# Two attentions of a four-layer kernel: the dilated shift moved into spare rows of the queries, and weighted sums turned by transpositions

## The chip, the cores and the metric

The kernel runs on one core of one Trainium2 chip. The core has five instruction streams that run side by side: PE (TensorE, which multiplies matrices; its loads of the standing operand are listed as PEld), DVE (VectorE), ACT (ScalarE), POOL (GpSimd) and SP (SyncE, which here only issues transfers). The metric is the device time of one execution in microseconds (us); lower is better.

## The reference, cut to what matters

The input is x with 8 batches of 512 tokens of 128 numbers. Four layers follow, each added to x. The first and the third are attentions with 16 heads of 8 numbers:

```python
# layer 1 (called "w" in the kernel): three attentions over the same q, k, v, averaged
o_loc = attention within windows of 128 tokens
o_dil = attention among the tokens i, i+4, i+8, ... (DIL = 4 phases of 128 tokens)
o_glb = attention over all 512 tokens
o = (o_loc + o_dil + o_glb) / 3 @ w_out
# layer 3 (called "c"): q and k rotated (RoPE), causal attention over 512 tokens
```

Layers 2 and 4 are mixtures of experts; the change doesn't touch them.

## The kernel before, in words

One function, `attention`, builds both attentions (`causal` False for the first, True for the second). A batch is cut into four groups of four heads; one group of one batch is a slot, and there are 32 slots in each attention. The order of the work inside a slot is written out by hand in `slot`, the same list for every engine: unit i (10 units in the first attention, 8 in the second) is one `scores` of that unit, then the products for maxima (`smax`) of a later slot, then whatever `put(i, ...)` places there. Every engine walks the list in order and waits on semaphores, so a late operand stops all that stands behind it on that engine.

**Queries and keys.** To keep precision in bf16, q and k are split into three bf16 parts each. `parts_out` writes the parts of a batch from SBUF to a scratch tensor in DRAM, and `stacks` reads them back so that the tiles QS and KS hold 72 rows (3 x 3 x 8) whose product is q times k. Rows 72 to 95 are zero. Rows 96 to 110 of QS hold the shifts (in three bf16 parts) that are taken off the scores before the exponential: for each window block and, as the fifth, for the dilated attention. KS rows 96 to 127 hold marks that pick the right shift row for a key block. `smax` multiplies rows 0 to 95 alone; DVE then takes the maxima, and `maxima` (DVE, POOL), `rows` (PE transposes them, ACT copies them to the tile MR, SP moves MR to QS rows 96 and on) make the shifts of the next slot. The first `scores` of a slot waits for that transfer (semaphore `s_ml`).

**Scores.** In the first attention units 0 to 7 multiply all 128 rows; units 8 and 9 make the dilated scores of two heads each: for each head one product of `dil_b` (a constant with ones at the fifth shift rows) with all of QS, 128x512, which lays the dilated shift down in PSUM, then four products of rows 0 to 95, 128x128 each, added to it.

**Sums.** `pv` multiplies exponentials by values into one PSUM bank, 32 rows a head: in the first attention the rows 10k to 10k+8 of a head are the eight sums and the denominator of kind k (local, dilated, global parts), in the second rows 0 to 8. `evac` (ACT) copies the bank to the tile OS. `sel` then turns it to tokens: PE multiplies OS by a constant `pick` (four float32 products of 108 columns in the first attention, 36 in the second), and DVE divides by the denominators and writes PR (POOL adds the three kinds) or ON.

**SP's order around the change.** In a slot with g = 1 of the first attention SP issues, one behind the other, `rows`, then `parts_out(b+1, 1)` (three transfers), and then, at the start of the slot with g = 2, `stacks(b+1, 0)` and `stacks(b+1, 1)` (six transfers each). PE needs the first of these stacks, for the next batch, at unit 4 of that same slot g = 2, in `smax` j = 0, which waits for `s_rd[0]`. The other groups' stacks are needed a slot or more later.

Of the kernel before, what the change touches and what calls it, by code (L numbers as in the profile page):

```python
# [13 lines left out]
P = 128  # L14
# [11 lines left out]
MR0 = 96  # L26

# [35 lines left out]
def attention(nc, X, const, w, scratch, causal, due=None, gate=None):  # L63
# [24 lines left out]
    with nc.cleanup_on_exit(), ExitStack() as ctx:  # L88
# [30 lines left out]
        if not causal:  # L119
            LW = sb("lw", [P, NT, HG * NT])  # L120
            GLB = sb("glb", [P, HG, NT])
            LOC = sb("loc", [P, HG, NT])
            DIF = sb("dif", [P, NG, HG * NT])
            E1 = sb("e1", [P, NG, HG * NT])
            T1 = sb("t1", [P, NT, HG])
            DEN = sb("den", [P, NT, HG])
            PR = sb("pr", [P, NT, KINDS * HG, DH])
# [3 lines left out]
        RL = sb("rl", [P, NT, KINDS * HG, 1])  # L131
# [44 lines left out]
        s_mark = sem("mark")  # L176
        NV = 1 if causal else 2
# [49 lines left out]
        SLOTS = B * NG  # L227

# [230 lines left out]
        def _(dve):  # L459
# [116 lines left out]
            def sel(n, g, b, turn):  # L576
                dve.wait_ge(s_full, turn + 1)
                k = KINDS * HG
                got = MI[:, 0:NT * k * OC].rearrange("p (t k c) -> p t k c", t=NT, k=k)
                if causal:  # L580
                    dve.reciprocal(RL[:, :, :, :], got[:, :, :, DH:OC]).then_inc(s_no, 1)
# [4 lines left out]
                    dve.tensor_tensor(out, got[:, :, :, 0:DH], RL[:, :, :, :].broadcast_to([P, NT, k, DH]), ALU.mult  # L586
                                      ).then_inc(s_no, 1)
                    return

                e1 = E1[:, g, :].rearrange("p (h t) -> p t h", h=HG)  # L590
                dve.wait_ge(s_e1, n + 1)
                dve.tensor_tensor(T1[:, :, :], e1, got[:, :, 0:HG, DH], ALU.mult).then_inc(s_no, 1)
                dve.reciprocal(RL[:, :, 0:2 * HG, :], got[:, :, 0:2 * HG, DH:OC]).then_inc(s_no, 1)
                dve.wait_ge(s_no, NNO * n + 1)
                dve.tensor_tensor(DEN[:, :, :], T1[:, :, :], got[:, :, 2 * HG:3 * HG, DH], ALU.add).then_inc(s_no, 1)
                dve.wait_ge(s_no, NNO * n + 3)
                dve.reciprocal(RL[:, :, 2 * HG:3 * HG, 0], DEN[:, :, :]).then_inc(s_no, 1)
                dve.wait_ge(s_no, NNO * n + 4)
                dve.tensor_tensor(T1[:, :, :], e1, RL[:, :, 2 * HG:3 * HG, 0], ALU.mult).then_inc(s_no, 1)
                dve.wait_ge(s_no, NNO * n + 5)  # L600
                dve.tensor_tensor(RL[:, :, 0:HG, 0], RL[:, :, 0:HG, 0], T1[:, :, :], ALU.add).then_inc(s_no, 1)
                dve.wait_ge(s_no, NNO * n + 6)
                if n:
                    dve.wait_ge(s_on, 2 * n)
                dve.tensor_tensor(PR[:, :, :, :], got[:, :, :, 0:DH], RL[:, :, :, :].broadcast_to([P, NT, k, DH]), ALU.mult
                                  ).then_inc(s_no, 1)
# [112 lines left out]
        def _(pe):  # L719
# [71 lines left out]
            def scores(n, g, b, turn, i):  # L791
# [6 lines left out]
                if i == 0:  # L798
                    pe.wait_ge(s_ml, 16 * (n + 1))
# [104 lines left out]
        def _(act):  # L904
# [92 lines left out]
            def rows(n, g, b, turn):  # L997
                act.wait_ge(s_full, turn + 1)
                if n:
                    act.wait_ge(s_ml, 16 * n)  # L1000
# [45 lines left out]
        def _(pool):  # L1046
# [99 lines left out]
            def sel(n, g, b, turn):  # L1146
# [6 lines left out]
                pool.tensor_tensor(out, PR[:, :, 0:HG, :], PR[:, :, HG:2 * HG, :], ALU.add).then_inc(s_on, 1)  # L1153
                pool.wait_ge(s_on, 2 * n + 1)
                pool.tensor_tensor(out, out, PR[:, :, 2 * HG:3 * HG, :], ALU.add).then_inc(s_on, 1)
# [59 lines left out]
        def _(sp):  # L1215
# [3 lines left out]
            def parts_out(b, turn, side):  # L1219
                if b:  # L1220
                    sp.wait_ge(s_pt[side], NPT * (b + 1))
                if side == 0 and b >= 2:
                    for g in range(NG):
                        sp.wait_ge(s_rd[g], 16 * 2 * SPLIT * (b - 1))
# [8 lines left out]
            def stacks(b, turn, g):  # L1233
# [3 lines left out]
                rows_ = SPLIT * DH  # L1237
                if b == 0:
# [11 lines left out]

            def rows(n, g, b, turn):
# [3 lines left out]
                sp.dma_start(QS[MR0:MR1, g * HG:(g + 1) * HG, :], MR[:, :]).then_inc(s_ml, 16)  # L1255

# [29 lines left out]
            walk(sp, dict(parts_out=parts_out, stacks=stacks, rows=rows, loads=loads, finish=finish))  # L1286


def constants():
# [6 lines left out]
    pick = np.zeros((P, 3, HG, OC), np.float32)  # L1296
    for k in range(3):
        for h in range(HG):
            for c in range(OC):
                pick[h * VW + KC * k + c, k, h, c] = 1.0  # L1300
    marks = np.zeros((P, NT), np.float32)
    dil = np.zeros(P, np.float32)
    for i in range(SPLIT):
        at = MR0 + i * (NT + 1)
        marks[at:at + NT] = np.eye(NT)
        dil[at + NT] = 1.0
# [4 lines left out]
        "dil": np.tile(dil[:, None], (1, P)),  # L1311
# [4 lines left out]
        "pick": pick.reshape(P, 3 * HG * OC),  # L1316
# [21 lines left out]
def setup(nc, ctx, c_dram, at, x_dram, X, w0qkv, w0out, w1qkv, w1out, w1rot, s_late):  # L1338
# [5 lines left out]
    CB = sb("const_b", [P, 5 * P], BF16)  # L1344
# [7 lines left out]
    for i, name in enumerate(("ident", "ones", "before", "dil", "later")):  # L1352
# [13 lines left out]
    with nc.cleanup_on_exit(), ExitStack() as inner:  # L1366
# [13 lines left out]
        def _(dve):  # L1380
            dve.wait_ge(s_c, 16)
            for i, name in enumerate(("ident", "ones", "before", "dil", "later")):
# [1098 lines left out]
```

## Time and profile before

| what | value |
|---|---|
| time, median of 3 runs | 1562.77 us (1562.21 to 1564.46) |
| span of the profiled execution | 1558.4 us |
| PE busy | 1394.4 us (89%) |
| DVE busy | 1064.0 us (68%) |
| ACT busy | 897.1 us (58%) |
| POOL busy | 657.4 us (42%) |

Times of a trace count from the start of the profiled execution, whose span is 4.4 us below the median run; what lies around the span is not in the trace. The first attention lies between about 6 and 608 us, the second between about 960 and 1396 us. A line such as L864 is a line of the kernel before. Busy time of PE is the union of its products, whose ends are modelled, so the distance from one product's start to the next one's start is the better measure of what a product takes up.

### The profile page before, as it was taken

The page shows a single profiled execution, that of the slowest core. Times are in us where ns is not written, and L with a number is a line of the kernel's source. Part 1 is how long each engine was busy: PE and PEld are TensorE (multiplying, and loading weights), DVE is VectorE, ACT ScalarE, POOL GpSimd, SP SyncE. Part 2 cuts the span into 40 slices and gives each one's busy share as a digit, 9 for nine tenths or more (in the row PEclk, how much of TensorE's full clock was granted, in tenths as well). Part 3 has the DMA queues.
Part 4 walks back from the last instruction along what each step waited for, and adds up shares of the span by engine and source line. Part 5 has one row for each costly group of instructions (what it writes and reads, how often), then busy time and mean ns, then how long its engine had stood idle before and what let it go on. Part 6 is the DMA issues. An engine that isn't in the chain of part 4 may idle for free. (4 is left out here: it accounts for less than half of the span.)

```text
span 1558.4 us, 36906 instructions
## 1 busy us (share of the span) xinstructions
PE 1394.4 (89%) x12642; PEld 923.9 (59%) x12642; DVE 1064.0 (68%) x2705; ACT 897.1 (58%) x1595; POOL 657.4 (42%) x985
## 2 busy tenths in 40 slices
PE   5899999999999997998999992799999999973976
PEld 2355555555555554766999991255555555543976
DVE  4877878787877763674444444678887887845767
ACT  3567676767767665631444440356756666651766
POOL 4223242323423222056333317566668554252756
PEclk7799999999999998998999995699999999985988
DMA  5111211212121102260111112433433332313763
GB/s 173 32 52 43 63 51 39 58 35 71 30 62 47 58 7 90 86 98 11 47 49 49 49 39 32 109 74 72 127 70 100 75 85 69 91 39 110 255 179 96
DMA packets 91880, 113.78 MB, mean 73 GB/s; under 512 B 13107, under 2 KB 75474, under 8 KB 91698
## 3 DMA queue, kind: packets, MB, share of 16 engines
q1 hardware_dynamic: 74170, 88.74, 20.2%
q0 software_dynamic: 16736, 21.55, 5.8%
q8 instruction: 106, 1.74, 0.5%
q10 hardware_dynamic: 792, 1.12, 0.3%
q14 instruction: 76, 0.62, 0.1%
HBM read 71.91 MB, written 38.95 MB: 71 GB/s over the span
## 5 line engine op out<-in xcount | busy, mean ns | idle before, releaser
L533 DVE TENSOR_REDUCE wm<-wsm 128x16 f32<-128x512 f32 x512 | 330.4, 685 | 110.2 <-PE wsm L781 107.1
L974 ACT ACTIVATE we<-wst 128x1024 f32<-128x1024 f32 x320 | 325.2, 1023 | 116.2 <-PE wst L814 105.6
L529 DVE TENSOR_REDUCE cnm<-csm 128x1 f32<-128x512 f32 (+3 forms) x352 | 213.6, 637 | 46.8 <-PE csm L778 44.4
L974 ACT ACTIVATE ce<-cst 128x896 f32<-128x896 f32 (+1 forms) x256 | 173.5, 699 | 111.6 <-PE cst L809 76.9
L781 PE MATMUL wsm<-wks,wqs 96*128 96x512 bf16 x512 | 173.5, 394 | 10.2 <-DVE wm L533 6.5
L814 PE MATMUL wst<-wqs,wks 128*128 128x512 bf16 x512 | 149.8, 384 | 0.3 <-ACT we L974 0.2
L774 PE MATMUL csm<-cks,cqs 96*128 96x256 bf16 (+3 forms) x512 | 131.5, 309 | 12.6 <-DVE cnm L529 9.6
L2067 PE MATMUL abup<-abxt,abws 128*128 128x128 f32 x1120 | 139.3, 278 | 0.4 <-ACT abxt L2093 0.4
L2067 PEld LDWEIGHTS abup<-abxt,abws 128*128 128x128 f32 x1120 | 133.3, 195 | 0.7 <-ACT abxt L2093 0.7
L848 PE MATMUL woa<-we,wv 128*32 128x128 f32 (+2 forms) x2560 | 130.5, 340 | 0.0
L1084 POOL TENSOR_TENSOR wdif<-wglb,wloc 128x16 f32<-128x16 f32 x32 | 7.1, 222 | 287.8 <-DVE wloc L555 287.8
L806 PE MATMUL cst<-cqs,cks 128*128 128x512 bf16 (+3 forms) x512 | 118.7, 301 | 0.7 <-ACT ce L974 0.7
L2115 DVE TENSOR_TENSOR abht<-absg,abup 128x512 f32<-128x512 f32 x70 | 48.1, 687 | 102.4 <-ACT absg L2098 102.4
L2131 POOL DMA_INDIRECT axb<-rows,asource x67 | 66.3, 990 | 117.7 <-DVE abys L2122 113.4
L1163 POOL TENSOR_SCALAR_AFFINE_SELECT ce<-ce 128x256 f32<-128x256 f32 x128 | 65.2, 543 | 88.9 <-ACT ce L974 88.4
L781 PEld LDWEIGHTS wsm<-wks,wqs 96*128 96x128 bf16 x512 | 49.7, 98 | 88.9 <-DVE wm L533 50.5
L2098 ACT ACTIVATE absg<-abup 128x512 f32<-128x512 f32 x70 | 41.8, 597 | 103.8 <-PE abup L2067 103.8
L848 PEld LDWEIGHTS woa<-we,wv 128*32 128x32 f32 x2560 | 66.8, 109 | 53.1 <-issue 36.6
L774 PEld LDWEIGHTS csm<-cks,cqs 96*128 96x128 bf16 x512 | 45.5, 101 | 74.3 <-DVE cnm L529 43.7
L778 PE MATMUL csm<-const_b 128*128 128x128 bf16 (+2 forms) x352 | 87.9, 250 | 0.0
L840 PE MATMUL coa<-ce,cv 128*32 128x512 f32 (+3 forms) x1024 | 82.2, 439 | 1.7 <-POOL ce L1163 1.0
L814 PEld LDWEIGHTS wst<-wqs,wks 128*128 128x128 bf16 x512 | 39.7, 101 | 63.6 <-issue 26.2
(321 smaller groups left out, 3007.4 us busy)
## 6 DMA issues: line engine op xcount, KB each, us to landing
wqs<-qk_parts SPq DMA_DIRECT2D x96, 96.0 KB
cqs<-qk_parts SPq DMA_DIRECT2D x96, 96.0 KB
wks<-qk_parts SPq DMA_DIRECT2D x93, 96.0 KB
cks<-qk_parts SPq DMA_DIRECT2D x93, 96.0 KB
br<-rows SPq DMA_DIRECT2D x39, 194.0 KB, 2.8
qk_parts<-wpt SPq DMA_DIRECT2D x48, 128.0 KB
qk_parts<-cpt SPq DMA_DIRECT2D x48, 128.0 KB
br<-rows SPq DMA_DIRECT2D x39, 130.0 KB, 2.8
```

Source lines behind the costliest of these rows:

```text
L529: dve.tensor_reduce(NM[:, n % 2, first:first + heads, t], got, AX.X, ALU.max).then_inc(s_mx, 1)
L533: dve.tensor_reduce(M[:, n % 2, hs, t, :].rearrange("p (w f) -> p w f", f=DIL), SM[:, j % 2, :].rearrange("p (w i f) -> p w f i", w=NT, f= ...
L774: pe.matmul(sm[:, i * keys:(i + 1) * keys], QS[0:MR0, h, t * P:(t + 1) * P], KS[0:MR0, h, 0:keys], start=(i == 0), stop=False, skip_group_ ...
L778: pe.matmul(own, const["later_b"], ident, start=False, stop=True, skip_group_check=True).then_inc(s_sm, 1)
L781: pe.matmul(sm, QS[0:MR0, h, t * P:(t + 1) * P], KS[0:MR0, h, :], start=True, stop=True, skip_group_check=True).then_inc(s_sm, 1)
L806: m = pe.matmul(st[:, at:at + width], KS[:, h, kb * P:(kb + 1) * P], QS[:, h, kb * P:S], start=True, stop=not masked, skip_group_check=True)
L814: m = pe.matmul(st[:, c * S:(c + 1) * S], KS[:, h, kb * P:(kb + 1) * P], QS[:, h, :], start=True, stop=True)
L840: m = pe.matmul(OA[VW * hs:VW * (hs + 1), S - width:S], V[:, kb, g * HG + hs, 0:VW], E[:, e_slot(g, HG * r + hs), at:at + width], start=(k ...
L848: m = pe.matmul(span(OA[VW * hs:VW * (hs + 1), :], a, z), V[:, r, g * HG + hs, col:col + VW], span(e, a, z), start=(r == 0 and a == 0), st ...
L974: act.activation(E[:, e_slot(g, i), 0:width], ST[:, (U * g + i) % 2, 0:width], ACT.Exp, scale=SCALE).then_inc(s_ex, 1)
L2067: m = pe.matmul(UP[:, i % 2, w, c * P:(c + 1) * P], WS[:, i % 2, w, c * P:(c + 1) * P], XT[:, i % 2, :], start=True, stop=True)
L2131: pool.indirect_dma_start(XB[:, q, :], None, rows, bass.IndirectOffsetOnAxis(ap=source[:, i:i + 1], axis=0)).then_inc(s_in[q], 16)
```

## The change

1. First attention: QS rows 72 to 74 now hold the three parts of the dilated shift and KS rows 72 to 74 hold ones, so that the four 128x128 products of a head already take the shift off. The 128x512 product with `dil_b` is gone. Units 0 to 7 multiply the same rows, so every score of a query there is shifted by one more number, which the division by the sums takes out again.
2. `rows` on SP issues three more transfers in each slot of the first attention: for each part, four rows of MR (one for each head) to one row of QS. `s_ml` now counts all four.
3. The rows 72 to 74 must be zero when the next batch's `smax` reads them: `stacks` issues, for b >= 1, one more transfer ahead of the others, from the zero rows 75 to 77 to 72 to 74; `s_rd` counts it.
4. SP lays the ones into KS once, ahead of the first stacks (`ones`); the first `smax` waits for it.
5. Both attentions: `sel` on PE is four transpositions of OS (128x128, with the identity) in place of the products with `pick`. DVE and POOL read the sums where they lie, with a step of 32 between heads; the number of their operations and of their elements is the same.
6. The constants `dil` and `pick` (236 columns of float32) are gone from the first load, and one of five casts.

```diff
+DR0 = SPLIT * SPLIT * DH
...
+        def loaded(b):
+            return 16 * (2 * SPLIT * (b + 1) + (0 if causal else b))
+        SHIFT_LOADS = 16 if causal else 16 * (1 + SPLIT)
...
             def smax(n, g, b, turn, j):
                 if j == 0:
-                    pe.wait_ge(s_rd[g], 16 * 2 * SPLIT * (b + 1))
+                    pe.wait_ge(s_rd[g], loaded(b))
+                    if n == 0 and not causal:
+                        pe.wait_ge(s_dilmark, 16)
...
                 if i == 0:
-                    pe.wait_ge(s_ml, 16 * (n + 1))
+                    pe.wait_ge(s_ml, SHIFT_LOADS * (n + 1))
...
-                        pe.matmul(st[:, at:at + S], const["dil_b"], QS[:, h, :], start=True, stop=False, skip_group_check=True)
                         for t in range(NT):
                             m = pe.matmul(st[:, at + t * P:at + (t + 1) * P], KS[0:MR0, h, t::DIL],
-                                          QS[0:MR0, h, t * P:(t + 1) * P], start=False, stop=(t == NT - 1),
+                                          QS[0:MR0, h, t * P:(t + 1) * P], start=(t == 0), stop=(t == NT - 1),
                                           skip_group_check=True)
...
             def sel(n, g, b, turn):
                 pe.wait_ge(s_ev, n + 1)
-                c = KINDS * HG * OC
                 for t in range(NT):
-                    m = pe.matmul(MI[:, c * t:c * (t + 1)], OS[:, g % 2, t * P:(t + 1) * P], const["pick"][:, 0:c],
-                                  start=True, stop=True, skip_group_check=True)
+                    m = pe.transpose(MI[:, t * P:(t + 1) * P], OS[:, g % 2, t * P:(t + 1) * P], const["ident"])
                 m.then_inc(s_full, 1)
...
             (DVE, sel)
-                got = MI[:, 0:NT * k * OC].rearrange("p (t k c) -> p t k c", t=NT, k=k)
+                wide = MI[:, :].rearrange("p (a e) -> p a e", e=VW)
...
             (SP, stacks)
+                if b and not causal:
+                    sp.dma_start(QS[DR0:DR0 + SPLIT, heads, :], QS[DR0 + SPLIT:DR0 + 2 * SPLIT, heads, :]).then_inc(s_rd[g], 16)
...
+            def ones(b, turn, which):
+                if causal or which == 0:
+                    return
+                sp.wait_ge(s_ones, 2)
+                ones_ = const["ones_b"][0:SPLIT, :].rearrange("p (a k) -> p a k", a=1).broadcast_to([SPLIT, H * S // P, P])
+                sp.dma_start(KS[DR0:DR0 + SPLIT, :, :].rearrange("p h (a k) -> p (h a) k", k=P), ones_).then_inc(s_dilmark, 16)
...
             (SP, rows)
                 sp.dma_start(QS[MR0:MR1, g * HG:(g + 1) * HG, :], MR[:, :]).then_inc(s_ml, 16)
+                if not causal:
+                    for a in range(SPLIT):
+                        own = (a * SHIFTS + NT) * HG
+                        sp.dma_start(QS[DR0 + a:DR0 + a + 1, g * HG:(g + 1) * HG, :], MR[own:own + HG, :]).then_inc(s_ml, 16)
```

## Rows read from the trace of the kernel before

**Rows 1.** The page: span, and the clock granted to PE, in tenths, in 40 slices.

```profile
span 1558.4 us, 36906 instructions
...
PEclk7799999999999998998999995699999999985988
```

**Rows 2.** Windows of both attentions: busy us of each engine, PE's clock, DMA share, GB/s.

```profile
118.80:513.00 394.20, 391.01 (x4173) 217.90 (x4173) 310.01 (x680) 280.83 (x354) 128.65 (x283) 1.00 0.18 51
1020.00:1390.00 370.00, 350.37 (x3206) 206.28 (x3209) 293.46 (x735) 239.11 (x423) 213.96 (x296) 1.00 0.31 83
```

**Rows 3.** Groups by line, 0 to 640 us: the shift products, and sel's.

```profile
L819 PE MATMUL wst<-wqs,const_b 128*128 128x512 bf16 x128 | 48.8, 381 | 1.3 <-ACT we L974 1.3
...
L864 PE MATMUL wmi<-const,wos 128*128 128x108 f32 x256 | 33.4, 273 | 0.8 <-ACT wos L981 0.8
```

**Rows 4.** Timeline of PE, two slots (start us, us, engine, line, operation, count).

```profile
342.52 0.60 PE L871 MATMUL wmi<-const,won 128*128 128x128 f32 x4
342.96 0.38 PE L819 MATMUL wst<-wqs,const_b 128*128 128x512 bf16 x1
...
353.43 1.04 PE L864 MATMUL wmi<-const,wos 128*128 128x108 f32 x8
354.31 0.59 PE L814 MATMUL wst<-wqs,wks 128*128 128x512 bf16 x2
...
358.89 0.38 PE L819 MATMUL wst<-wqs,const_b 128*128 128x512 bf16 x1
359.11 0.39 PE L821 MATMUL wst<-wqs,wks 96*128 96x128 bf16 x4
...
361.10 0.83 PE L781 MATMUL wsm<-wks,wqs 96*128 96x512 bf16 x2
...
362.87 0.60 PE L814 MATMUL wst<-wqs,wks 128*128 128x512 bf16 x2
```

**Rows 5.** Timeline of DVE in the second of these slots (in brackets, idle before).

```profile
357.78 2.00 DVE L533 TENSOR_REDUCE wm<-wsm 128x16 f32<-128x512 f32 x3 [0.58 <-PE wsm L781]
360.20 2.61 DVE L533 TENSOR_REDUCE wm<-wsm 128x16 f32<-128x512 f32 x4 [0.41 <-PE wsm L781]
```

**Rows 6.** Timeline of SP's transfers in the same slot and the next.

```profile
359.09 0.92 SPq L1255 DMA_DIRECT2D wqs<-wmr  x1
360.06 1.84 SPq L1230 DMA_DIRECT2D qk_parts<-wpt  x3
362.00 2.30 SPq L1243 DMA_DIRECT2D wqs<-qk_parts  x3
364.35 1.25 SPq L1249 DMA_DIRECT2D wks<-qk_parts  x3
```

**Rows 7.** Timeline of PE's weight loads at unit 4, g = 2, one batch earlier.

```profile
301.64 0.16 PEld L781 LDWEIGHTS wsm<-wks,wqs 96*128 96x128 bf16 x2 [0.27 <-DMA wks<-qk_parts]
```

**Rows 8.** Lines of SP: time to issue one transfer, ns, min/median/max.

```profile
L1255 SPq DMA_DIRECT2D cqs<-cmr x32: 709/755/807, 999.8 to 1378.1; - x32
...
L1249 SPq DMA_DIRECT2D wks<-qk_parts x93: 296/365/2053, 26.9 to 538.5; - x93
...
L1266 SPq DMA_DIRECT2D bb<-L_ffn_b x1: 287/287/287, 1107.7 to 1107.7; - x1
```

**Rows 9.** Transfers: KB each, median us from issue to landing.

```profile
art<-L_ffn_router_w SPq DMA_DIRECT2D x1, 3.5 KB, 2.3
```

**Rows 10.** Timeline of PE around sel in the second attention.

```profile
1197.09 1.03 PE L864 MATMUL cmi<-const,cos 128*128 128x36 f32 x8
1197.96 0.68 PE L752 MATMUL cst<-cxnT,w1r 128*128 128x512 f32 x1
```

**Rows 11.** Waits in the second attention, 1020 to 1390 us (total, times, longest).

```profile
PEld csm L774 <- DVE cnm L529: 32.7, 80, 1.1
...
PEld csm L774 <- DMA cks<-qk_parts: 0.8, 2, 0.5
```

**Rows 12.** Timeline of PE: its first product for maxima.

```profile
31.38 1.04 PE L781 MATMUL wsm<-wks,wqs 96*128 96x512 bf16 x2 [0.26 <-DMA wks<-qk_parts]
```

More of the change, by code:

```diff
@@ L126, in attention @@
             DEN = sb("den", [P, NT, HG])
-            PR = sb("pr", [P, NT, KINDS * HG, DH])
+            PR = sb("pr", [P, NT * HG, KINDS, DH])
         MT = sb("mt", [P, NT, MROWS], BF16)
@@ L130, in attention @@
         OS = sb("os", [P, 2, S])
-        RL = sb("rl", [P, NT, KINDS * HG, 1])
+        RL = sb("rl", [P, NT * HG, KINDS, 1])
         ON = sb("on", [P, NT, D])
@@ L176, in attention @@
         s_mark = sem("mark")
+        s_dilmark = sem("dilmark")
         NV = 1 if causal else 2
@@ L585, in sel @@
                     out = ON[:, :, g * HG * DH:(g + 1) * HG * DH].rearrange("p t (h c) -> p t h c", h=HG)
-                    dve.tensor_tensor(out, got[:, :, :, 0:DH], RL[:, :, :, :].broadcast_to([P, NT, k, DH]), ALU.mult
-                                      ).then_inc(s_no, 1)
+                    got = wide[:, :, 0:DH].rearrange("p (t h) c -> p t h c", h=HG)
+                    dve.tensor_tensor(out, got, RL[:, :, 0, :].rearrange("p (t h) a -> p t h a", h=HG).broadcast_to(
+                        [P, NT, HG, DH]), ALU.mult).then_inc(s_no, 1)
@@ L588, in sel, with den, inverse @@
                     return
+                got = wide[:, :, 0:KINDS * KC].rearrange("p a (k c) -> p a k c", c=KC)
+                def den(k):
+                    return got[:, :, k, DH].rearrange("p (t h) -> p t h", h=HG)
+                def inverse(k):
+                    return RL[:, :, k, 0].rearrange("p (t h) -> p t h", h=HG)
                 e1 = E1[:, g, :].rearrange("p (h t) -> p t h", h=HG)
                 dve.wait_ge(s_e1, n + 1)
-                dve.tensor_tensor(T1[:, :, :], e1, got[:, :, 0:HG, DH], ALU.mult).then_inc(s_no, 1)
@@ L593, in sel @@
-                dve.reciprocal(RL[:, :, 0:2 * HG, :], got[:, :, 0:2 * HG, DH:OC]).then_inc(s_no, 1)
+                dve.tensor_tensor(T1[:, :, :], e1, den(0), ALU.mult).then_inc(s_no, 1)
+                dve.reciprocal(RL[:, :, 0:2, 0], got[:, :, 0:2, DH]).then_inc(s_no, 1)
                 dve.wait_ge(s_no, NNO * n + 1)
-                dve.tensor_tensor(DEN[:, :, :], T1[:, :, :], got[:, :, 2 * HG:3 * HG, DH], ALU.add).then_inc(s_no, 1)
+                dve.tensor_tensor(DEN[:, :, :], T1[:, :, :], den(2), ALU.add).then_inc(s_no, 1)
@@ L1152, in sel @@
                 out = ON[:, :, g * HG * DH:(g + 1) * HG * DH].rearrange("p t (h c) -> p t h c", h=HG)
-                pool.tensor_tensor(out, PR[:, :, 0:HG, :], PR[:, :, HG:2 * HG, :], ALU.add).then_inc(s_on, 1)
+                kind = PR[:, :, :, :].rearrange("p (t h) k c -> p t h k c", h=HG)
+                pool.tensor_tensor(out, kind[:, :, :, 0, :], kind[:, :, :, 1, :], ALU.add).then_inc(s_on, 1)
                 pool.wait_ge(s_on, 2 * n + 1)
-                pool.tensor_tensor(out, out, PR[:, :, 2 * HG:3 * HG, :], ALU.add).then_inc(s_on, 1)
+                pool.tensor_tensor(out, out, kind[:, :, :, 2, :], ALU.add).then_inc(s_on, 1)
             def scores(n, g, b, turn, i):
@@ L1223, in parts_out @@
                     for g in range(NG):
-                        sp.wait_ge(s_rd[g], 16 * 2 * SPLIT * (b - 1))
+                        sp.wait_ge(s_rd[g], loaded(b - 2))
                 for a in range(SPLIT):
@@ L1284, in finish @@
                 sp.wait_ge(s_pad, 16 * NE1)
-            walk(sp, dict(parts_out=parts_out, stacks=stacks, rows=rows, loads=loads, finish=finish))
+            walk(sp, dict(parts_out=parts_out, ones=ones, stacks=stacks, rows=rows, loads=loads, finish=finish))
 def constants():
@@ L1295, in constants @@
     angle = np.outer(freqs[(p % DH) // 2], np.arange(S, dtype=np.float32)).astype(np.float32)
[L1296 to L1300, printed above, removed]
     marks = np.zeros((P, NT), np.float32)
-    dil = np.zeros(P, np.float32)
     for i in range(SPLIT):
@@ L1305, in constants @@
         marks[at:at + NT] = np.eye(NT)
-        dil[at + NT] = 1.0
     parts = {
@@ L1310, in constants @@
         "before": np.where(p[:, None] < p[None, :], np.float32(1), np.float32(0)),
-        "dil": np.tile(dil[:, None], (1, P)),
         "later": np.where(p[:, None] > p[None, :], -big, np.float32(0)),
@@ L1315, in constants @@
         "marks": marks,
-        "pick": pick.reshape(P, 3 * HG * OC),
         "minus_half": np.full((P, B * NT), -0.5, np.float32),
@@ L1343, in setup @@
     C = sb("const", [P, c_dram.shape[1]])
-    CB = sb("const_b", [P, 5 * P], BF16)
+    CB = sb("const_b", [P, 4 * P], BF16)
     W0 = sb("w0", [P, 3 * D])
@@ L1351, in setup @@
     const["late"] = s_late
-    for i, name in enumerate(("ident", "ones", "before", "dil", "later")):
+    for i, name in enumerate(("ident", "ones", "before", "later")):
         const[name + "_b"] = CB[:, i * P:(i + 1) * P]
@@ L1381, in _ @@
             dve.wait_ge(s_c, 16)
-            for i, name in enumerate(("ident", "ones", "before", "dil", "later")):
+            for i, name in enumerate(("ident", "ones", "before", "later")):
                 dve.tensor_copy(CB[:, i * P:(i + 1) * P], const[name]).then_inc(s_cb, 1)
```

13 lines of the change are left out of this document (6 added, 7 removed).

## The prediction, made before the changed kernel was run

> **What bounds the kernel now.** I read the page first: PE's clock digits are 9 through most of both attentions, 7 at the very start [rows 1]. The windows then show PE busy in 391.0 of 394.2 us of the first attention and in 350.4 of 370.0 us of the second, with DVE at 79% in both [rows 2]. So PE sets the pace of both, DVE is the next wall, and the work that the change takes off PE counts unless something else becomes late. The question is then what stands close behind PE at the places that the change shortens, and I went through one slot of the first attention engine by engine.
>
> The reader should see three near misses there. First, in the dilated units DVE rests for 0.41 us only [rows 5]. Second, the transfer of the shifts is issued at 359.09 us and the first scores of the next slot start at 362.87, 3.78 us later [rows 4, 6]. Third, the stack of keys for the next batch comes just in time: one batch earlier PE's load waited 0.27 us for it, although PE lost nothing by it [rows 7]. The last two hang on SP, which issues from 359.09 to 365.6 us without a rest [rows 6], and the change gives SP more to issue.
>
> **The sums turned, first attention.** Four products with pick are eight instructions and take PE from 353.43 to 354.31, 0.88 us; 256 such records are the 32 slots [rows 3, 4]. Four transpositions of the same size, of another tile, are four instructions and take from 342.52 to 342.96, 0.44 us [rows 4]. That is 0.44 us a slot, 32 slots: -14.1 us. What follows on PE is a scores and pv, none of which waited there, so I count it all. DVE's and POOL's operations stay in number and elements; a larger step between elements costs nothing in my sum, and if it cost 0.1 us an operation DVE's slack before unit 6 (0.58 us idle [rows 5]) would cover it.
>
> **The shift product.** Each takes PE 0.22 us (358.89 to 359.11), four a slot, 128 in all [rows 3, 4]: 0.88 us a slot if PE alone counted. It doesn't: in units 8 and 9 DVE takes four maxima back to back in 2.61 us and the last maxima product, the second of 361.10, must wait for one of them [rows 4, 5]. Without the shift products DVE can begin those four 0.41 us sooner, its rest before them, and no more. So the next slot's first scores could come 0.41 us sooner, at 359.09 + 3.37.
>
> **The shift transfers.** They are the unknown. SP would issue three more after the first, whose issue takes 0.92 us [rows 6]. The trace has no such transfer (four rows of one tile to four pieces of one row). Its neighbours: 0.755 us for 12 rows of the same tile to three rows, 0.365 for 24 plain rows, 0.287 for one row [rows 8]. The first is nearest in kind, the last in size; I take 0.50, midway between 0.287 and 0.755, and 0.04 between issues (359.09 + 0.92 to 360.06 leaves 0.05 [rows 6]). From the end of an issue to landing: a transfer of 3.5 KB lands 2.3 us after the start of its issue [rows 9], so with an issue of 0.3 to 0.9 that is 1.4 to 2.0; I take 1.4, since these stay inside SBUF, and 0.06 to PE. The last one lands at 0.92 + 3 x 0.54 + 1.4 + 0.06 = 4.0 us after 359.09. PE now comes at 3.78 and would come at 3.37. So the next slot starts 0.22 us later than now: the shift products' gain is gone and a little more. In one slot of four `heads_T` (0.44 us [rows 4]) and the output product stand between too, and there the 0.41 stays. Sum: 24 x 0.22 - 8 x 0.41 = +2.0 us.
>
> **The stacks.** Behind `rows` at g = 1 stand parts_out and the six transfers of the first stack [rows 6]; parts_out starts at once when `rows` is issued, so three issues of 0.54 delay it all, and the clearing transfer, a plain one, adds 0.44 (0.365 and its gaps [rows 8]): 2.06 us. The key stack is just in time [rows 7]; I give it 0.2 us of slack. PE, meanwhile, arrives 0.22 us later. PE then stands still at unit 4 of g = 2 for 2.06 - 0.22 - 0.2 = 1.64 us a batch. The prologue loads batches 0 and 1 in another order, so six batches: +9.8 us. The other stacks are wanted a slot later, and no slot is so short that 2 us matter.
>
> **The start.** The first product for maxima waits for stacks [rows 12]. The transfer of ones is issued just ahead of them, 192 pieces of 256 bytes: one issue (0.3 to 0.8 us) and some transfer time, +1.0 us. A first load that is 236 columns shorter and one cast less: -0.4 us.
>
> **The second attention.** Its pick products take 1197.09 to 1197.96, 0.87 us [rows 10], so a transposition saves 0.43 us a slot, 13.8 us in 32. No transfer is added there. PE's loads wait for DVE for 32.7 us in all, and twice for a key stack [rows 11]: a tenth of the slots already have PE behind another, and a stack that is just in time gives back up to 0.4 us in each of seven batches. I take 3 us off: -10.8 us.
>
> **Sum.** -14.1 + 2.0 + 9.8 + 0.6 - 10.8 = -12.5 us. The profiled span is 1558.4 us [rows 1] and the median 1562.8, 4.4 us above it; I take these 4.4 as unchanged: 1550 us.
>
> **A rule that bears on the issues.** The Trainium skill ("DMA: Bandwidth & Descriptors", section "Anatomy of one DMA", the table on where the 2 us go) gives a sequencer's dispatch as about 50 ns and the generation of descriptors as small. By it an added transfer would cost SP next to nothing: an estimate from that page is 4 x 0.05 = 0.2 us before the stacks, and some 1528 us in all. The trace disagrees for every form that it has, 0.287 to 0.92 us [rows 6, 8], so I go by the rows.
>
> **Rivals.**
> (a) The issue is cheap, 0.29 us. For: one row, one piece, as the 0.287 row [rows 8]. Then the last shift lands 3.37 us after 359.09, when PE comes: all 32 slots keep 0.41, -13.1 in place of +2.0. The stacks are 3 x 0.33 + 0.33 = 1.3 us later and PE 0.41 sooner: 1.5 x 6 = +9.1. In all -28: 1534 us. Chance 0.22.
> (b) The issue is as dear as the nearest in kind, 0.755 us. Then the shift lands 4.77 us after 359.09: 24 slots are 0.99 us longer (+23.8), the others gain nothing; stacks 3.2 - 0.99 - 0.2 = 2.0, x 6 = +11.9. With -14.1, +0.6 and -10.8: +11, 1574 us, slower. Each us of issue price costs 24 x 3 + 6 = 78 us, so the sign turns at 0.50 + 12.5/78 = 0.66 us. Chance 0.17.
> (c) The stacks are not later, because their landing hangs on the transfers in flight and not on SP's issue. Against: the chain of issues has no gap [rows 6]. 1550 - 9.8 = 1540 us. Chance 0.10.
> (d) The second attention gives nothing, because DVE, 79% busy, takes PE's place there. 1550 + 10.8 = 1561 us, no change. Against: PE is 95% busy there [rows 2]. Chance 0.07.
> (e) PE's clock falls. In the trace it stays at full in windows full of transpositions and stalls [rows 1, 2]. Half speed in a tenth of the second attention would cost 37 us x 0.5 = 18 us: 1568 us. Chance 0.02. The Trainium skill ("TensorE: Matmul & The Clock Gate", Part 4) says that transpositions don't count as PE's activity as other products do; by it this would be likelier, but four transpositions are 0.44 us of a slot that is over 9 us long [rows 4].
>
> **How the numbers follow.** My forecast, 1550 us, has 0.42, with a range of its own of 1543 to 1558 (an issue of 0.41 to 0.60 us). The range for all: the ends of the issue price give 1534 and 1574; rivals (c) and (d) lie inside; leaving out the last of (b), 1532 to 1572. A measurement tells 0.2%, 3.1 us, from no change: faster is below 1559.6. Faster: 0.42 + 0.22 + 0.10 less a little for the forecast's own upper end = 0.72. Same: (d) and issue prices of 0.62 to 0.70 us, 0.11. Slower: (b), (e), 0.17.
>
> **What would show it.** In the changed trace: sel's four instructions take about 0.44 us in both attentions; no 128x512 product in the dilated units; SP's issues of the new transfers, whose price decides between (a), the forecast and (b); PE's load for the first scores of a slot waiting for the transfer from MR (0.6 us a slot in three of four by the forecast, none by (a), 1.4 by (b)); its load at unit 4 of g = 2 waiting some 1.6 us for `wks`; and the first product for maxima at about 32 us. The prediction is wrong if the new transfers' issue lies outside 0.4 to 0.6 us, or if their landing takes much more than 1.4 us after it, which costs 24 us for each further us.

## The result, and the profile after

| kernel | median | runs |
|---|---|---|
| before | 1562.58 us (1561.5 to 1564.46) | 10 |
| after | 1558.57 us (1552.65 to 1563.65) | 10 |

The ratio is 0.9976, with an interval of 0.9966 to 0.9986: 4.0 us faster, where 12.5 were forecast. The runs of the changed kernel scatter over 11 us, those of the kernel before over 3 here, and over 5 to 6 in the comparisons further down. The profiled run of after is its slowest (1563.65 us, span 1561.9), so its trace is read for places and prices, and the times come from the medians. In the runs below a time lies 1.7 us above its span.

The page of after: span, and the clock granted to PE, in tenths, in 40 slices.

```profile
span 1561.9 us, 36109 instructions
...
PEclk7799999999999997999999996699999999986988
```

Windows of after: both attentions, and three stretches of one batch (start and end, length, then busy us of PE, PEld, DVE, ACT, POOL with their counts, PE's clock, DMA share, GB/s).

```profile
118.80:513.00 394.20, 358.14 (x3914) 194.22 (x3984) 306.90 (x672) 274.69 (x349) 125.58 (x276) 0.99 0.17 50
1020.00:1390.00 370.00, 343.33 (x3116) 196.06 (x3146) 301.74 (x747) 244.31 (x432) 220.60 (x302) 1.00 0.32 83
...
290.00:303.40 13.40, 10.88 (x113) 6.90 (x115) 7.63 (x15) 8.37 (x12) 2.44 (x7) 1.00 0.28 80
303.80:310.60 6.80, 5.22 (x33) 2.64 (x37) 3.52 (x10) 1.02 (x1) 1.36 (x6) 0.50 0.34 91
310.80:316.00 5.20, 4.71 (x51) 2.42 (x47) 3.75 (x6) 3.99 (x5) 0.30 (x2) 1.00 0.04 13
```

Against [rows 2] PE is no longer the engine without rest: it is busy in 358.1 us of 394.2 where it was in 391.0. It had less work, but the attention hardly got shorter.

Timeline of PE in after, one batch (start us, us, engine, line, operation, count; in brackets how long PE rested before it, and for what).

```profile
305.38 1.03 PE L798 MATMUL wsm<-wks,wqs 96*128 96x512 bf16 x2 [3.41 <-DMA wks<-qk_parts]
306.21 1.06 PE L879 MATMUL wmi<-const,wos 128*128 128x128 f32 x4
...
324.40 0.60 PE L879 MATMUL wmi<-const,wos 128*128 128x128 f32 x4
324.84 0.60 PE L831 MATMUL wst<-wqs,wks 128*128 128x512 bf16 x2
...
328.77 0.61 PE L831 MATMUL wst<-wqs,wks 128*128 128x512 bf16 x2
329.80 0.39 PE L798 MATMUL wsm<-wks,wqs 96*128 96x512 bf16 x1 [0.42 <-DVE wm L541]
330.02 0.61 PE L837 MATMUL wst<-wqs,wks 96*128 96x128 bf16 x8
330.47 0.91 PE L798 MATMUL wsm<-wks,wqs 96*128 96x512 bf16 x2
...
333.86 0.38 PE L831 MATMUL wst<-wqs,wks 128*128 128x512 bf16 x1 [0.23 <-DMA wqs<-wmr]
```

The four transpositions take 0.44 us (324.40 to 324.84), as forecast, and two heads' dilated products stand in one row of eight with no 128x512 product. Three new rests stand beside them: for DVE at unit 7 (0.42 us), for the shifts' transfer (0.23), and for the stack of keys (3.41). Within the last the clock fell to half, at 303.8 us, and stayed there for 6.8 us; the four transpositions at 306.21 took 0.85 us (to 307.06) instead of 0.44.

Timeline of SP in after.

```profile
363.61 0.92 SPq L1279 DMA_DIRECT2D wqs<-wmr  x1
364.57 1.91 SPq L1283 DMA_DIRECT2D wqs<-wmr  x3
366.52 1.86 SPq L1245 DMA_DIRECT2D qk_parts<-wpt  x3
368.43 0.77 SPq L1254 DMA_DIRECT2D wqs<-wqs  x1
369.24 2.20 SPq L1260 DMA_DIRECT2D wqs<-qk_parts  x3
371.48 1.25 SPq L1266 DMA_DIRECT2D wks<-qk_parts  x3
```

Its two new kinds of issue, by line (ns, min/median/max, first and last start).

```profile
L1283 SPq DMA_DIRECT2D wqs<-wmr x96: 572/584/701, 51.2 to 593.0; - x96
...
L1254 SPq DMA_DIRECT2D wqs<-wqs x28: 702/714/770, 84.5 to 545.1; - x28
```

One of the new transfers costs 0.584 us of SP, 0.65 with its gap ((1.91 + 0.04) / 3). In [rows 6] the stacks of queries began 2.91 us after `rows`; here it is 5.63 (363.61 to 369.24).

Waits of after, 118.8 to 500 us (total us, times, longest), and last one of its second attention, 1020 to 1390 us.

```profile
PEld wsm L798 <- DMA wks<-qk_parts: 11.0, 5, 3.9
...
PE wst L831 <- DMA wqs<-wmr: 9.6, 16, 0.9
PE wsm L798 <- DMA wks<-qk_parts: 8.6, 5, 3.4
...
PEld csm L791 <- DVE cnm L537: 36.0, 86, 1.5
```

Timeline of PE in after: its first product for maxima.

```profile
32.45 1.03 PE L798 MATMUL wsm<-wks,wqs 96*128 96x512 bf16 x2 [1.61 <-DMA wqs<-qk_parts]
```

PE itself now waits 18.2 us for the two transfers in this stretch; in the kernel before only its loads waited for a stack, 0.27 us where shown [rows 7]. In the second attention the loads wait 36.0 us for DVE in place of 32.7 [rows 11]. The kernel before began its first product for maxima at 31.38 [rows 12], so the start costs 1.1 us by these two traces.

**A measure for the experiments.** DVE reads 16 maxima tiles a slot; from the first read of one slot to that of the next is a slot's length. The first read of a slot falls in unit 4 two slots ahead. The table gives, from each kernel's trace, the median over the batches from the second on (the range, where it scatters), by the group g whose unit 4 begins the stretch. A single fall of PE's clock lengthens the stretch that it hits: in after, stretches 2 to 3 of 18.37 and 17.46 us stand beside four of 16.1.

| kernel (us) | 2 to 3 | 3 to 0 | 0 to 1 | 1 to 2 (stacks) |
|---|---|---|---|---|
| before | 16.26 | 16.40 | 18.76 | 18.29 |
| after | 16.11 | 16.07 | 17.92 | 19.2 to 22.0 |
| sums alone | 15.93 | 16.42 | 18.34 | 18.11 |
| no shift product | 15.82 | 15.97 | 18.35 | 17.9 to 18.2 |
| transfers alone | 16.52 in three batches, 17.8 to 18.2 in three | 16.49 | 18.76 | 20.0 to 21.5 |
| one transfer | 15.39 | 15.98 | 17.92 | 17.7 to 19.6 |
| sums turned, no product, no transfers | 15.41 | 15.98 | 17.94 | 17.7 to 18.8 |

### The profile page after: what moved, and what is told of

Same layout as the page of the kernel before. It is cut to its first block and busy times, and to the rows that moved or that the text cites. A ratio compares the mean times of both kernels' runs of the same rounds, so it can differ in the third digit from the quotient of the medians.

```text
span 1561.9 us, 36109 instructions
## 1 busy us (share of the span) xinstructions
PE 1340.1 (86%) x12132; PEld 880.4 (56%) x12258; DVE 1063.7 (68%) x2704; ACT 891.3 (57%) x1595; POOL 656.5 (42%) x985
## 5 line engine op out<-in xcount | busy, mean ns | idle before, releaser
L988 ACT ACTIVATE we<-wst 128x1024 f32<-128x1024 f32 x320 | 319.1, 1022 | 131.9 <-PE wst L831 129.8
L798 PE MATMUL wsm<-wks,wqs 96*128 96x512 bf16 x512 | 181.3, 399 | 31.9 <-DVE wm L541 13.2
L831 PE MATMUL wst<-wqs,wks 128*128 128x512 bf16 x418 | 131.0, 390 | 27.1 <-DMA wqs<-wmr 17.5
L823 PE MATMUL cst<-cqs,cks 128*128 128x384 bf16 (+3 forms) x480 | 111.8, 295 | 2.7 <-ACT ce L988 0.7
```

Of the source, the lines that this page charges most:

```text
L823: m = pe.matmul(st[:, at:at + width], KS[:, h, kb * P:(kb + 1) * P], QS[:, h, kb * P:S], start=True, stop=not masked, skip_group_check=True)
L831: m = pe.matmul(st[:, c * S:(c + 1) * S], KS[:, h, kb * P:(kb + 1) * P], QS[:, h, :], start=True, stop=True)
L988: act.activation(E[:, e_slot(g, i), 0:width], ST[:, (U * g + i) % 2, 0:width], ACT.Exp, scale=SCALE).then_inc(s_ex, 1)
```

## The experiments

**1. The sums alone** (`e1_sums_only`). The kernel before with `sel` as in the change in both attentions; the shift product stays, and no transfer is added.

> The kernel before with only the sums turned by transpositions, in both attentions; shift product and transfers as before. By the terms of the prediction (0.44 and 0.43 us a slot, 32 slots each, 3 us given back) it is 25 us faster, 1538 us. If DVE takes PE's place in the second attention, only the first gains: 14 us, 1549 us. If neither attention is held by PE at that place: no change, 1562.5 us.

1545.1 us (1544.2 to 1547.9), ratio 0.9888 (0.9872 to 0.9903): -18.4 us, not -25. The table says where: the stretch 3 to 0 gained nothing, and 1 to 2 only 0.18 us. The timeline of PE in the kernel before at unit 7 of that slot:

```profile
323.19 0.60 PE L814 MATMUL wst<-wqs,wks 128*128 128x512 bf16 x2
323.77 0.39 PE L781 MATMUL wsm<-wks,wqs 96*128 96x512 bf16 x1
```

The same place in this kernel:

```profile
318.76 0.60 PE L829 MATMUL wst<-wqs,wks 128*128 128x512 bf16 x2
319.80 0.39 PE L796 MATMUL wsm<-wks,wqs 96*128 96x512 bf16 x1 [0.43 <-DVE wm L541]
```

And DVE's timeline there:

```profile
317.29 0.68 DVE L541 TENSOR_REDUCE wm<-wsm 128x16 f32<-128x512 f32 x1
317.89 0.86 DVE L476 BATCH_NORM_STATS2 wstats<-X 128x6 f32<-128x128 f32 x4
318.78 0.38 DVE L479 BATCH_NORM_AGGREGATE wmv<-wstats 128x2 f32<-128x6 f32 x4
319.08 1.85 DVE L541 TENSOR_REDUCE wm<-wsm 128x16 f32<-128x512 f32 x3
```

From scores to the maxima product it is 0.58 us before and 1.04 here. DVE's chain (the sums, a read, `norm_stats` of 1.2 us, a read) already set the pace at that place, and gave back all that the transpositions had saved. The larger step between elements is not the reason: DVE's operations on the sums take what they took (the last one 557 ns against 558, the two reciprocals 349 and 254 against 346 and 253).

**2. No shift product** (`e2_no_product`). The kernel before without the 128x512 product; the dilated shift is left out of the scores, and no transfer is added.

> The kernel before without the product with dil_b, and with none of the new transfers; it leaves the dilated shift out. If DVE's four maxima in units 8 and 9 are the limit, 0.41 us a slot: 13 us faster, less up to 2 us at the key stack, 1550 to 1552 us. If PE alone counts, 0.88 us a slot: 28 us faster, 1534 us. If DVE hides the product wholly: 1562 us.

1551.2 us (1548.6 to 1553.2), ratio 0.9921 (0.9907 to 0.9935): -12.3 us, as expected. Three of the four stretches are 0.41 to 0.44 us shorter, the one with the stacks 0.07 to 0.44.

**3. The transfers alone** (`e3_transfers_only`). The kernel before, with the three transfers of every slot and the clearing; the product stays.

> The kernel before with the new transfers of the shift parts (three a slot) and the clearing transfer added and waited for, product with dil_b kept, no ones in KS, so that the added rows meet zeros. With the issue price of the changed kernel's trace (0.58 us and gaps) the first scores of 24 slots wait 0.5 us (+12 us) and the key stack 2 us in six batches (+12 us): 1586 us, and more if PE's clock falls in these waits. If SP's issues are hidden: 1562.5 us. If only the stacks wait: 1577 us.

1586.3 us (1585.7 to 1587.4), ratio 1.0144 (1.0128 to 1.0159): +22.8 us. Its waits, 118.8 to 500 us:

```profile
PE wsm L787 <- DMA wks<-qk_parts: 9.7, 5, 2.6
PE wst L820 <- DMA wqs<-wmr: 6.2, 16, 0.9
```

The last column grows by 1.7 to 3.2 us a batch, and the rest for the stack, 1.9 us a batch, is the most of it. The stretch 2 to 3 grows by 0.26 us in three batches and by 1.6 to 1.9 in the three others, where PE's clock had fallen at the rest for the stack; the other two grow by 0.09 and 0. Windows of this kernel on the three falls:

```profile
166.30:169.70 3.40, 3.14 (x12) 2.42 (x13) 1.69 (x5) 0.00 (x0) 0.00 (x0) 0.50 0.42 118
313.10:316.50 3.40, 3.27 (x12) 2.41 (x13) 1.78 (x6) 0.00 (x0) 0.02 (x1) 0.50 0.36 108
459.80:463.20 3.40, 3.40 (x24) 2.23 (x26) 2.75 (x10) 0.87 (x1) 0.00 (x0) 0.51 0.20 82
```

**4. No clearing** (`e4_no_clear`). The changed kernel; `smax` multiplies rows 0 to 71, so nothing need be cleared.

```diff
-                if b and not causal:
-                    sp.dma_start(QS[DR0:DR0 + SPLIT, heads, :], ...).then_inc(s_rd[g], 16)
...
-                    pe.matmul(sm, QS[0:MR0, h, t * P:(t + 1) * P], KS[0:MR0, h, :], start=True,
+                    pe.matmul(sm, QS[0:KR, h, t * P:(t + 1) * P], KS[0:KR, h, :], start=True,
```

> The changed kernel with the products for maxima of the first attention reading rows 0 to 71, so that no clearing transfer is needed. If SP's issues ahead of the key stack are what PE waits for, each batch saves the 0.75 us of that issue: 4 to 6 us below the changed kernel, 1553 to 1555 us, or 8 to 10 us below if PE's clock also stops falling there. If the stack's time hangs on the transfers in flight: no change, 1558.5 us.

1559.7 us (1555.7 to 1563.1), ratio 0.9975 (0.9965 to 0.9986): as the changed kernel, a miss. In the trace the stacks were issued 4.9 us after `rows` in place of 5.63, but the key stack landed on average 9.0 us after its first issue where it had been 8.7. PE's waits for it fell from 8.6 to 7.4 us in five batches, too little to be seen in runs that scatter over 7 to 11 us.

**5. One transfer in place of three** (`e5_one_transfer`). As 4, and the shift's rows in MR in the order window, part, head, so that the dilated shift's 12 rows lie together.

```diff
+                    own = SPLIT * NT * HG
+                    sp.dma_start(QS[MR0:MR0 + SPLIT * NT, g * HG:(g + 1) * HG, :], MR[0:own, :]).then_inc(s_ml, 16)
+                    sp.dma_start(QS[DR0:DR0 + SPLIT, g * HG:(g + 1) * HG, :], MR[own:own + SPLIT * HG, :]).then_inc(s_ml, 16)
```

> The changed kernel with the rows of the shifts reordered (window, part, head), so that the dilated shift's three parts go in ONE transfer instead of three, and without the clearing transfer (its rows lie where nothing stale is read). Theory (the new transfers cost because SP issues them one after another, 0.58 us and a gap of 0.06 each, and the queue loads wait behind them): the last shift is issued some 1.3 us earlier, so the first scores of a slot no longer wait for it; the stacks of a batch are 4 x 0.65 = 2.6 us of SP's issue late instead of 7 or so, of which the 1.7 to 2 us of slack hide most. So the kernel falls to about 1544 us (1540 to 1550). Rival 1 (the landings are late because more transfers are in flight, not because of the issues): one landing in four is left of the new ones, and the stalls before the first maxima of a batch keep more than half of their length; 1550 to 1556. Rival 2 (neither; the spare rows themselves cost): stays at 1558.

1537.8 us (1532.9 to 1540.6), ratio 0.9825 (0.9806 to 0.9844): 25 us faster than before, and below the range expected. SP's timeline:

```profile
350.60 0.86 SPq L1283 DMA_DIRECT2D wqs<-wmr  x1
351.50 0.77 SPq L1284 DMA_DIRECT2D wqs<-wmr  x1
352.31 1.87 SPq L1247 DMA_DIRECT2D qk_parts<-wpt  x3
354.29 2.20 SPq L1260 DMA_DIRECT2D wqs<-qk_parts  x3
```

Twelve rows cost 0.77 us where four cost 0.58: most of the price is by the transfer. The last shift lands 3.1 us after `rows` is issued, where it was 4.0, and the first stack is issued at 3.69 us.

**6. That transfer on ACT's queue** (`e6_act_issues`). As 5, but ACT issues the second transfer, behind its copy to MR.

> As the kernel with one transfer for the dilated shift, but this transfer is issued by ACT, so that SP issues what it issued before the change. Theory (SP's queue): no stall is left before the first maxima of a batch beyond those of the kernel before, and the time is that of the sums and of the left-out product together, about 1535 us (1530 to 1541). Rival 1 (ACT's work is near the limit too, and 0.6 to 0.7 us of issue in each of 32 slots lands on the path): 1545 to 1560. Rival 2 (transfers in flight): no better than the kernel in which SP issues the one transfer.

1552.0 us (1549.5 to 1553.7), ratio 0.9925 (0.9911 to 0.9940). Rival 1 held. The stretches 2 to 3 and 0 to 1 are 16.07 and 18.88 us, 0.7 and 1.0 longer than in 5. ACT's timeline:

```profile
356.40 0.59 ACT L1015 ACTIVATE wmr<-wmi 60x512 bf16<-60x512 bf16 x1
357.02 0.75 ACTq L1021 DMA_DIRECT2D wqs<-wmr  x1
357.88 2.85 ACT L988 ACTIVATE we<-wst 128x1024 f32<-128x1024 f32 x3 [0.89 <-PE wst L837]
```

Its waits, 118 to 500 us; experiment 5 has no such wait there:

```profile
PE wst L837 <- ACT we L988: 11.1, 21, 0.8
```

ACT stands for 0.75 us ahead of the exponentials of the dilated units, and PE then waits for ACT to free PSUM. An issue is paid by whatever stands behind it.

**7. The sums in the first attention alone** (`e7_sums_first`). As 1, but the second attention keeps `pick`.

> The kernel before, with the sums turned by transpositions in the first attention alone; the second keeps its products with the pick matrix. By the traces of the kernel with both turned, the first attention gives 6.7 us and the second 6.1: 1563.5 - 6.7 = about 1557 us (1554 to 1559). By my prediction's terms the first gives 14.1: 1549. If the rest between the 12.8 of the traces and the 18.4 measured belongs to the first attention: 1551.

1553.5 us (1553.2 to 1555.1), ratio 0.9940 (0.9924 to 0.9955): -9.3 us, more than the 6.7 read from traces, and short of the other two numbers expected (1551 and 1549 us). The first attention's sums are worth 9.3 us, the second's the remaining 9.1 of experiment 1; the intervals allow either number some 2 to 3 us.

**8. norm_stats elsewhere** (`e8_stats_early`). As 1, with one line of the written order moved.

```diff
                 if g == 2:
+                    put(0, "norm_stats", b + 2)
...
                 if g == 3:
-                    put(5, "norm_stats", b + 2)
```

> The kernel with the sums turned by transpositions (first experiment, 1545.1 us), with norm_stats of the batch after the next moved from slot 3, unit 5 to slot 2, unit 0. Theory (in slot 3 DVE's chain of sums, reads and norm_stats is the limit, and gives back all of the 0.45 us that TensorE saves there): 0.4 us in each of 7 batches comes free, 1542 us (1540.5 to 1543.5). Rival (DVE isn't the limit in slot 3; something behind the transpositions is): 1545 as before. If norm_stats is now in the way of slot 2: 1546 to 1549.

1544.6 us (1543.6 to 1547.1), ratio 0.9878 (0.9861 to 0.9896): 0.5 us less than experiment 1, not told apart from no change, where 3 were expected. The place of the timeline above, in this kernel:

```profile
318.79 0.60 PE L829 MATMUL wst<-wqs,wks 128*128 128x512 bf16 x2
319.24 0.38 PE L796 MATMUL wsm<-wks,wqs 96*128 96x512 bf16 x1
```

The rest of 0.43 us is gone. The stretch 3 to 0 is 15.82 us (-0.60) and 1 to 2 is 18.30 (+0.19): by the trace 0.41 us a batch, as expected, and 2.9 us from the first read of the first attention to that of its last slot (520.1 against 523.0 us). The profiled run, the slowest of four, lost 4.6 us in the second attention instead, where PE's clock was at half for 6.8 us from 1020.6. So the cause in slot 3 is shown; its worth in the median isn't, by this run alone.

**9. Experiments 5 and 8 together** (`e9_both`).

> The changed kernel with the dilated shift's rows in one transfer (1537.8 us so far) and norm_stats of the batch after the next moved out of slot 3 to slot 2, unit 0. In the kernel with the sums alone this move took 2.8 us out of the first attention (first to last read of maxima 533.8 against 536.6 us) and 0.5 us off the median. Theory (DVE in that slot): 2 to 3 us less here too, about 1535 us. Rival (with the shift product gone DVE is behind in slot 2 as well, and the move only moves the loss): 1537 to 1539.

1533.1 us (1531.8 to 1535.8), ratio 0.9811 (0.9796 to 0.9826), the fastest kernel here that leaves nothing out. The stretch 3 to 0 is 15.39 us, all others as in 5. It is 4.7 us below experiment 5 by the medians, 2.2 us by the ratios (the intervals overlap).

**10. Sums turned, no product, no transfers** (`e10_sums_no_product`). The dilated shift is left out.

> The kernel before with the sums turned by transpositions in both attentions and the dilated shift's product left out; no transfer is added, so the dilated shift is missing from the result. If the two savings add up (-18.4 and -12.3): 1532 us, and the one added transfer costs 5.8 us of the kernel with one transfer. Rival (both draw on the same DVE time, and don't add): 1535 to 1538, and that transfer costs next to nothing.

1532.7 us (1532.3 to 1534.5), ratio 0.9804 (0.9790 to 0.9818), against 1564.2 for the kernel before beside it: -31.6 us, and 18.4 + 12.3 is 30.7. The two savings add up. Experiment 5, which adds the ones and one transfer a slot, lies 5 us above it. The first product for maxima in this kernel:

```profile
30.35 1.03 PE L796 MATMUL wsm<-wks,wqs 96*128 96x512 bf16 x2
```

**11. Three transfers in slot 1** (`e11_three_at_one`). As 5, but `step = 1 if g == 1 else SPLIT` rows a transfer.

> The kernel with one transfer for the dilated shift (1537.8 us), but in slot 1 of each batch, ahead of the stacks, it goes in three as in the changed kernel; the other slots keep one. Issued from SP some 1.3 us more before six of the stacks, and nothing else. Theory (the stacks land 8 to 10 us after their issue whatever is in flight, and PE had about nothing left to wait with): 1.2 us a batch, 6 x 1.2 = +7 us and perhaps a fall of the clock, 1545 to 1549. Rival (the loss is in the first scores of a slot that wait for the last shift, three slots in four, and the stacks matter little): 1538 to 1541.

1537.6 us (1535.9 to 1539.3), ratio 0.9828 (0.9814 to 0.9842): no change, but the edit was put in the wrong place. `rows(n + 1)` is issued a slot early, so those ahead of the stacks are the rows of g = 2. The three of g = 1 fell where SP rests, and there they cost nothing.

**12 and 13. Three transfers ahead of the stacks, and in all other slots** (`e12_three_ahead`: `g == 2`; `e13_three_elsewhere`: `g != 2`).

> The kernel with one transfer for the dilated shift (1537.8 us), but in slot 2 alone it goes in three: that is the transfer that SP issues just ahead of parts_out and the first stacks (the three transfers of the kernel before it were issued one slot too early, in SP's rest). SP comes to the stacks 1.2 us later, six times. Stack theory: the stalls before the first maxima product of a batch grow from 0.65 to 1.9 us, 6 x 1.2 = +7 us, and 2 to 5 more where the clock falls behind them: 1545 to 1550. Rival (the loss of the changed kernel lies in the first scores that wait for the last shift): 1538 to 1540.

> The complement: three transfers in slots 0, 1 and 3, one in slot 2. The stacks are issued as in the kernel with one transfer. In the changed kernel PE waited for the last shift 9.6 us in 5.5 batches, 1.75 us a batch, in three slots of four. Slot 1 alone cost nothing. If the others bear the waits and slot 2 had its share: 2/3 of 14 us, +9, 1547 us (1543 to 1550). If nearly all of the 22 us between the changed kernel and that with one transfer belong to the stacks and the clock behind them: 1538 to 1541.

12: 1548.0 us (1544.5 to 1549.1), ratio 0.9907 (0.9893 to 0.9921), 10.1 above experiment 5, as expected. 13: 1542.9 us (1540.4 to 1547.9), ratio 0.9884 (0.9868 to 0.9901), 5.0 above, between the two ranges expected. SP's timeline in 12:

```profile
357.00 0.86 SPq L1286 DMA_DIRECT2D wqs<-wmr  x1
357.90 1.93 SPq L1289 DMA_DIRECT2D wqs<-wmr  x3
359.87 1.86 SPq L1250 DMA_DIRECT2D qk_parts<-wpt  x3
361.83 2.24 SPq L1263 DMA_DIRECT2D wqs<-qk_parts  x3
```

And PE's, at the first maxima product of two batches:

```profile
300.44 0.60 PE L801 MATMUL wsm<-wks,wqs 72*128 72x512 bf16 x2 [3.23 <-DMA wks<-qk_parts]
...
371.35 0.60 PE L801 MATMUL wsm<-wks,wqs 72*128 72x512 bf16 x2 [1.63 <-DMA wks<-qk_parts]
```

In 12 the stacks come 4.83 us after `rows` instead of 3.69, in six batches, and only the last column grows (18.9 to 21.6), but for one stretch 2 to 3 of 17.0 us behind the fall of the clock at 301.8. In 13 the last column is that of 5, and only 2 to 3 grows, from 15.39 to 16.02. So the stacks are the larger part, and of the first scores that wait only those of one slot in four cost time.

## Why the prediction was wrong

**Where it failed.** The sign held, and so did most of the mechanisms; the size didn't. The step that failed is "The sums turned, first attention", where it says: "What follows on PE is a scores and pv, none of which waited there, so I count it all." The saving itself was right, 0.44 us. But the argument looked only at what comes right behind `sel`, and a slot with g = 3 has a later place, unit 7, where DVE sets the pace. There the maxima product had stood 0.14 us behind its cover already (0.58 us for work of 0.44). The term of -14.1 us measured -9.3, and that of the second attention, -10.8, measured -9.1. Together -18.4 in place of -24.9: 6.5 of the 8.5 us by which the forecast of -12.5 missed. DVE's part in slot 3 is shown by experiment 8; what is missing in the stretches 2 to 3 (0.1 us) and 1 to 2 (0.26), and in the second attention (1.7 us in all, within what the intervals allow), is seen, but its cause was not tried. The signs that the prediction named for being wrong, the price of an issue (0.4 to 0.6 us; it is 0.584) and the landing behind it (1.4 us; it is 1.1), would have let it pass: neither looked at this term.

**The shift product**: right. The forecast allowed 0.41 us a slot, 13.1 us; experiment 2 gave 12.3, where PE's own 0.88 us would have given 28.

**The shift transfers**: the landing was right in sum, by errors that cancel. The landing of the last shift was put at 4.0 us after `rows`, and is at 3.99. But the issue takes 0.65 with its gap, not 0.54, and landing 1.1 us from its end, not 1.4. That this costs 24 slots was wrong: PE did wait in three slots of four (16 times in five and a half batches), but in one of them DVE was the limit anyway, and in another the stack's stall took the wait in. Of the 3.99 us, 2.87 are four issues. The Trainium skill ("DMA: Bandwidth & Descriptors", section "Anatomy of one DMA") puts most of a transfer's fixed time into the receipt at the target and about 50 ns into the dispatch, and its table is of transfers that GpSimd issues; the prediction applied it to SP. Of one transfer here, issued by SP, 1.1 us lie behind the issue, the larger part, as that page has it; but the issue is 0.58 us, and it is the issues that add up.

**The stacks**: mechanism right, too small. They come 2.72 us late, not 2.06 (three issues at 0.65 instead of 0.54, the clearing at 0.75 instead of 0.44), and the landing 8 to 10 us later keeps that. The rest was 1.9 us a batch in experiment 3 (9.7 in five), against 1.64. In five traces with one to four transfers a slot the key stack landed on average 8.7 to 9.1 us after its first issue, so rival (c), that landing hangs on what is in flight, falls.

**What the parts give together.** Sums and product together gave 31.6 us (experiment 10), where the prediction had 38.0 (14.1 + 10.8 + 13.1). From there the changed kernel loses about 27.6 us again to transfers and start (-4.0 against -31.6), where the prediction had 25.5 (13.1 + 2.0 + 9.8 + 0.6). So 6.4 of the 8.5 us are savings that were too large, and 2.1 are costs that were too small.

Experiments 1, 2 and 3 added up give -18.4 - 12.3 + 22.8 = -7.9 us, 4 us more than the changed kernel gained. The intervals of the four ratios together are about as wide, so part of it can be chance. Two things in the traces go the right way. The ones are in none of the three: the first product for maxima starts at 32.45 us in after, and at 30.21, 30.55 and 31.16 in experiments 1, 2 and 3. And the shift's transfer costs more once the product is gone, because PE then comes sooner and the landing doesn't: it lengthens the stretch 2 to 3 by 0.26 us on the kernel before (experiment 3, batches at full clock) but by 0.70 on experiment 10 (15.41 to 16.11), 0.44 us a batch. The clock is no explanation of this difference by these traces: from 60 us to the last read of maxima it stood at half for 10.2 us in after (6.8 from 303.8 and 3.4 from 518.8) and for the same 10.2 us in experiment 3. How the 4 us divide was not tried.

Between experiments 4 and 5 lie 22 us. Experiments 12 and 13 account for 15 of them by the medians, and for 22 of 23 by the ratios, each taken against the kernel before beside it; whether anything is left can't be told.

**The rivals.** (a) falls, the issue isn't 0.29 us. (b) had the right direction: 0.65 with its gap is midway between the forecast's 0.54 and (b)'s 0.80. By the forecast's own 78 us for each us of price that alone would be +8.6; it wasn't, because of the two slots above. (d) falls by experiments 1 and 7. (e) was priced for the second attention and for transpositions; the clock did fall in the first, at stalls: in after within a rest of 3.41 us, with 6.8 us at 0.50. The Trainium skill ("TensorE: Matmul & The Clock Gate", Part 1) says that an idle PE goes back to 1.2 GHz, and the trace agrees. Transpositions brought no fall: experiments 1 and 9 have them in every slot, and from 60 us to the last read of maxima the clock was full.

**The start**: forecast +0.6 us, measured 1.1. One trace can't tell it well: the first product for maxima comes at 31.8 to 32.9 us in the eight traces with the ones and at 30.2 to 31.5 in the seven without, and experiment 2, with all the old constants, has 30.55 among them. So the ones cost about 1.5 us, not 1.0, and the gain of the shorter load can't be seen.

## What to carry to other kernels

An engine that is 99% busy isn't the limit at every place: before a saving is counted as many times as there are slots, follow it through a whole slot to the next place where the engine meets another one, and look there for a rest that is already above zero. A small transfer costs the queue that issues it more by the transfer than by the byte (0.58 us for four rows, 0.745 for twelve); count what is queued behind it, lay out the rows so that one transfer does, and give it to no engine that is itself close to the limit. Of two errors that cancel only a test of each part tells. And a part's cost, measured alone, needn't be its cost in the whole: a transfer that PE just about meets costs more once PE is made faster.

## What the runs showed of the hardware that was not expected

Four rows of one tile to one row of another, inside SBUF, took 0.584 us to issue, twelve rows to three 0.745 on SP's queue and 0.73 on ACT's, and the transfer of ones (192 pieces) 0.93. No issue on SP's queue in the kernels before and after took less than 0.287 us. The row that was nearest in kind (0.755) was a better guide than the one nearest in size (0.287). The same stack landed anywhere from 7.9 to 10.1 us after its first issue, batch by batch, in the five traces named above. Each of the eight falls of the clock seen between 60 us and the first attention's last read of maxima came at a rest of PE for a stack: of 3.41 and 2.47 us in after, 2.56, 1.94 and 2.19 in experiment 3, 3.42 in 4, 1.60 in 5, 3.23 in 12, each with 3.4 or 6.8 us at half clock. Four other rests of 1.63 to 1.71 us had no fall. So a late transfer can cost more than its wait, and now and then rather than always, which fits the scatter of 11 us over the runs of the changed kernel; that the falls make this scatter isn't shown.
